# The ninth expert of a gated mixture: half of its tokens by seven block products instead of eight, and the last layers' work packed into fewer steps

## The reference, cut to what matters

```python
# layer 2: eight experts and a shared one, D = 256, F = 1024
g = einsum('bsd,edf->ebsf', h, Wg); u = einsum('bsd,edf->ebsf', h, Wu)
expert_outs = einsum('ebsf,efd->ebsd', silu(g) * u, Wd)
x2 = x + (1 - sg) * einsum('be,ebsd->bsd', probs, expert_outs) + sg * ((silu(h @ Sg) * (h @ Su)) @ Sd)
# layer 3: adapter of 64 hidden units, then a layer norm (weights picked by language)
z = x2 + relu(x2 @ w1 + b1) @ w2 + b2
x3 = x2 + (z - mean(z)) * rsqrt(var(z) + 1e-5) * gamma + beta
# layer 4: one matrix for each sequence
out = x3 + x3 @ W[subject].T + bias[subject]
```

## Time and profile before

| what | us |
|---|---|
| median of 3 runs (1583.22 to 1584.35) | 1583.36 |
| time of the profiled execution | 1581.01 |
| its span | 1579.2 |
| PE busy in the span | 1570.2 |
| DVE busy | 1133.2 |
| ACT busy | 931.4 |
| POOL busy | 671.3 |

### The profile page before, as it was taken

One profiled execution on the slowest core, in us unless ns is written; L12 is line 12 of the kernel. 1 busy time (PEld: TensorE's weight loads), 2 busy tenths in 40 slices (PEclk: granted clock), 3 DMA queues, 4 the chain that ended last, 5 costly groups with the idle time before them and its releaser, 6 DMA issues.

```text
span 1579.2 us, 22425 instructions
## 1 busy us (share of the span) xinstructions
PE 1570.2 (99%) x7916; PEld 1339.7 (85%) x7916; DVE 1133.2 (72%) x1685; ACT 931.4 (59%) x1683; POOL 671.3 (43%) x621
## 2 busy tenths in 40 slices
PE   9999999999999999999999999999999999999999
PEld 7888888999988888888888888888888888888898
DVE  6855556788889876777777776776776777657567
ACT  6655555666666665565666566656666666555444
POOL 7865544766787431432432442342342352038000
PEclk9999999999999999999999999999999999999999
DMA  4111105555520000010010010010010010022000
GB/s 161 56 53 54 54 27 179 169 183 177 171 83 31 20 34 27 14 41 27 15 40 28 14 41 27 14 40 28 14 41 27 14 41 27 15 59 77 14 14 28
DMA packets 31012, 85.98 MB, mean 54 GB/s; under 512 B 5030, under 2 KB 10534, under 8 KB 30774
## 3 DMA queue, kind: packets, MB, share of 16 engines
q1 hardware_dynamic: 30310, 83.21, 16.0%
q0 software_dynamic: 304, 1.10, 0.2%
q10 hardware_dynamic: 288, 0.26, 0.1%
HBM read 82.46 MB, written 2.10 MB: 54 GB/s over the span
## 4 chain that ended last, share of the span: by engine, by line
PE 93%; POOL 3%; issue 2%; DMA 0%; ACT 0%; DVE 0%; SPq 0%; POOLq 0%; ACTq 0%; DVEq 0%
PE up L682 13%; PE up L684 13%; PE up L683 13%; PE sum L441 12%; PE sum L442 12%; PE sum L443 12%; PE up L441 4%; PE up L442 3%; PE up L443 3%; PE up L450 2%; PE up L449 2%; PE up L451 2%; POOL expert_in L1496 1%; DMA raw<-in_shared 0%; POOL shared_up L1496 0%
## 5 line engine op out<-in xcount | busy, mean ns | idle before, releaser
L1305 ACT ACTIVATE hidden_hi<-up_tile 128x512 fp32r<-128x512 f32 x256 | 161.1, 629 | 189.2 <-DVE up_tile L2125 166.7
L2130 DVE TENSOR_TENSOR hidden_lo<-up_tile,hidden_hi 128x512 fp32r<-128x512 f32 x256 | 197.9, 792 | 44.7 <-ACT hidden_hi L1305 44.7
L2120 DVE TENSOR_TENSOR gate_tile<-up,gate_tile 128x512 f32<-128x512 f32 x192 | 130.1, 687 | 137.7 <-PE up L684 137.5
L441 PE MATMUL sum<-hidden_hi,down 128*128 128x512 f32 x512 | 199.2, 389 | 0.0
L443 PE MATMUL sum<-hidden_hi,down 128*128 128x512 f32 x512 | 199.2, 389 | 0.0
L442 PE MATMUL sum<-hidden_lo,down 128*128 128x512 f32 x512 | 199.2, 389 | 0.0
L683 PE MATMUL up<-x_sums,gate_up 128*128 128x512 f32 x512 | 199.2, 389 | 0.0
L682 PE MATMUL up<-x_sums,gate_up 128*128 128x512 f32 x512 | 199.2, 389 | 0.0
L684 PE MATMUL up<-x_sums,gate_up 128*128 128x512 f32 x512 | 199.2, 389 | 0.0
L2125 DVE TENSOR_TENSOR up_tile<-up_tile,gate_tile 128x512 f32<-128x512 f32 x192 | 184.0, 985 | 2.2
L1298 ACT ACTIVATE gate_tile<-gate_tile 128x512 f32<-128x512 f32 x192 | 119.9, 633 | 90.4 <-DVE gate_tile L2120 88.1
(11 more groups left out here) (332 smaller groups left out, 4004.9 us busy)
## 6 DMA issues: line engine op xcount, KB each, us to landing
raw<-in_experts SPq DMA_DIRECT2D x64, 512.0 KB, 3.3
raw<-in_l SPq DMA_DIRECT2D x51, 512.0 KB, 3.3
raw<-in_shared SPq DMA_DIRECT2D x23, 512.0 KB, 3.3
raw<-in_w SPq DMA_DIRECT2D x8, 256.0 KB, 2.6
x<-in_xT SPq DMA_DIRECT2D x3, 512.0 KB, 9.2
l_stage<-in_l SPq DMA_DIRECT2D x3, 512.0 KB, 4.2
out<-out_stage SPq DMA_DIRECT2D x6, 256.0 KB, 2.2
gate_w<-in_gw POOLq DMA_DIRECT2D x1, 1024.0 KB, 7.0
```

The source lines that it names most:

```text
L441: pe.matmul(out, wh, vh, start=start, stop=False)
L1305: A(hi[:, i], cu[:, i], ACT.Copy).then_inc(hi_done, 1)
L2120: V.tensor_tensor(t, ps, t, ALU.add).then_inc(c_done[m], 1)
L2130: V.tensor_tensor(lo[:, i], cu[:, i], hi[:, i].bitcast(f32), ALU.subtract).then_inc(lo_done, 1)
```

## The change

The ninth expert's first 1024 tokens go as a seventeenth row of pairs (`PAIR_BLOCKS` gets `(8, 0)`), so that 16 of the 40 plain steps go away and 4 pairs come in. The plain steps that stay are one job of 512 tokens and two of 256 (24 steps), and they read the pair's weight tiles; the one block that the pairs do not keep as such is kept in `l21` (one cast more of 128 columns on ACT and two subtractions on POOL for each pair of tiles). The separate tiles `gul` and `dnl` and their preparation go away. Units 0 and 1 (tokens 0 to 1023) are complete when the pairs are, so their stages now begin in steps 2 and 3. `WHEN` is written anew: five units' stages lie in 24 steps and the ones behind. The late weights are cast in steps 1, 1, 3, 3, 4, 5, 6, 7 (`LATE_AT`), the centring of b2 (`center_b2`, `b2_stage`) moves from step 9 to step 3. SP loads the constants before the pairs of the ninth expert, the eight b1 and four of the biases ahead of the fourth late weight, and the other four biases after unit 1's adapter down. For the units of 512 tokens ACT forms both squares and DVE only adds them. y, squares and hidden tiles have two or three copies at new places, among them squares of unit 0 at the place where the row sum of unit 1 goes, so `row_sum` waits for the variance of unit 0; on POOL it and `rstd_stage(0)` stand in the loop over the late weights. Unit 1 uses the other PSUM banks.

```diff
-LAST_JOBS = [(0, BLK), (BLK, BLK), (2 * BLK, BLK), (3 * BLK, S), (3 * BLK + S, S)]
+LAST_JOBS = [(2 * BLK, BLK), (3 * BLK, S), (3 * BLK + S, S)]
+UNITS = [(0, BLK), (BLK, BLK)] + LAST_JOBS
+LAST_STEPS = 8 * len(LAST_JOBS)
...
+PAIR_BLOCKS = [(e, j) for e in range(NS) for j in range(2)] + [(NS, 0)]
+NSS = len(PAIR_BLOCKS) * PAIRS
+LATE_AT = [1, 1, 3, 3, 4, 5, 6, 7]
...
-    (9, 10, 11, 11, 11, 11, 12, 12, 12, 13, 13, 13, 13, 14, 14, 14, 15, 15, 16, 16, 17, 18),
-    (17, 18, 19, 19, 19, 19, 20, 20, 20, 21, 21, 21, 21, 22, 22, 22, 23, 23, 24, 25, 25, 26),
-    (25, 26, 27, 28, 28, 28, 30, 30, 30, 31, 32, 31, 32, 34, 34, 35, 35, 36, 38, 38, 39, 39),
-    (34, 34, 35, 35, 35, 35, 37, 37, 37, 38, 39, 39, 40, 41, 43, 43, 45, 45, 46, 48, 46, 50))]
+    (2, 2, 4, 4, 4, 4, 6, 6, 6, 7, 7, 7, 7, 8, 8, 9, 9, 10, 12, 12, 12, 13),
+    (3, 6, 8, 9, 9, 9, 11, 11, 11, 12, 13, 12, 13, 15, 15, 15, 16, 16, 18, 18, 19, 19),
+    (10, 11, 14, 15, 15, 15, 17, 17, 17, 18, 19, 18, 19, 21, 21, 21, 22, 22, 24, 24, 26, 27),
+    (18, 18, 20, 21, 21, 21, 23, 23, 23, 24, 25, 25, 25, 26, 27, 27, 29, 29, 30, 32, 30, 34))]
...
                 act.wait_ge(centered, DT * i + 1)
-                A(sq[:, 0, c], y[:, 0, c], ACT.Square).then_inc(sq_first, 1)
+                if i:
+                    act.wait_ge(var_done, i)
+                A(sq_of[i][:, 0, c], y_of[i][:, 0, c], ACT.Square)
+                act.wait_ge(centered, DT * (i + 1))
+                A(sq_of[i][:, 1, c], y_of[i][:, 1, c], ACT.Square).then_inc(sq_first, 1)
...
             for b in reversed(range(B)):
-                hooks.setdefault(late_step(b), []).insert(0, lambda b=b: late_hi(b))
-            hooks.setdefault(24, []).append(beta_hi_part)
+                hooks.setdefault(LATE_AT[b], []).insert(0, lambda b=b: late_hi(b))
+            hooks.setdefault(16, []).append(beta_hi_part)
...
             def row_sum(i):
 
                 b0, nb, t0, c0, n = unit(i)
-                pool.wait_ge(x2_done, DT * (i + 1))
...
+                for dt in range(DT):
+                    x2_ready(pool, i, dt)
+                pool.wait_ge(mean_done, i)
+                pool.wait_ge(var_done, 1)
+                G(xst[:], x[:, 0, t0:t0 + n], x[:, 1, t0:t0 + n], ALU.add).then_inc(xs_sum, 1)
...
             for b in range(B):
                 w3_plus_one(b)
+                if b == B - 1:
+                    row_sum_lo(1)
                 if b:
                     late_lo(b - 1)
+                if b == 6:
+                    row_sum(1)
+                    rstd_stage(0)
             late_lo(B - 1)
...
-            hooks.setdefault(9, []).append(center_b2)
+            hooks.setdefault(16, []).append(beta_lo_part)
+            hooks.setdefault(3, []).append(center_b2)
```

More of the change, by code:

```diff
@@ L63 @@
 del WHEN[0]["hid"]
-WHEN += [{"x2": 42, "up": 43, "hid": 44, "down": 45, "res": 46, "square": 46, "split": 47, "var": 47, "eps": 49,
-          "scaled": 48, "base": 51, "final": 52, "beta": 41}]
+WHEN += [{"x2": 26, "up": 27, "hid": 28, "down": 29, "res": 30, "square": 30, "split": 31, "var": 31, "eps": 33,
+          "scaled": 32, "base": 35, "final": 36, "beta": 25}]
 STAGES += ["split", "beta", "scaled", "base", "final"]
@@ L155, in build @@
     ws = [place(f"weight_sums{s}", [P, 2, 7 * P], f32, over=f"gate_up{s}", skip=7 * K1) for s in range(PAIRS)]
-    xst = place("x_row_sum", [P, BLK], f32, over="raw", skip=14336)
-    xsr = [place(f"x_row_sum_parts{r}", [P, 2, BLK], f32r, over="weights", skip=(12 - 4 * r) * K1) for r in range(2)]
+    xst = place("x_row_sum", [P, BLK], f32, over="weights", skip=14 * K1)
+    xsr = place("x_row_sum_parts", [P, 2, BLK], f32r, over="weights", skip=12 * K1)
     cg = place("gate_tile", [P, 3, BLK], f32, over="weights", skip=88 * K1)
@@ L282, in last_steps @@
         def last_steps(step, hooks):
-            for T in range(40):
+            for T in range(LAST_STEPS):
                 job = T // FT
@@ L774, in last_up @@
                         b = (0, 1, 3, 2)[f % 2 * 2 + dt]
-                        c = slice(b * P, (b + 1) * P)
-                        last = product(ps, gul[f // 2][:, 0, m, c], gul[f // 2][:, 1, m, c],
+                        wt = [l21[f // 2][:, h, m] if b == 3 else gu[f // 2][:, h, m, b * P:(b + 1) * P] for h in range(2)]
+                        last = product(ps, wt[0], wt[1],
                                        xh[:, dt, tok:tok + N], xl[:, dt, tok:tok + N], dt == 0, dt == DT - 1)
@@ L973, in _ @@
                 l0_block(tb)
[L974 to L977, removed]
+            for e, j in PAIR_BLOCKS:
+                for s in range(PAIRS):
+                    pair_up(e, j, s)
             hooks = placed({"up": l2_up_stage, "mean": mean_stage, "down": l2_down_stage, "var": var_stage,
@@ L995, in _ @@
             last_steps(last_step, hooks)
-            for T in range(40, 60):
-                if T < 42:
+            for T in range(LAST_STEPS, ALL_STEPS):
+                if T < LAST_STEPS + 2:
                     last_down(T - 2, S)
@@ L1365, in pair_tiles @@
                     weights(e, j, s)
[L1367 to L1370, removed]
+            for e, j in PAIR_BLOCKS:
+                for s in range(PAIRS):
+                    pair_tiles(e, j, s)
             tile_hi(NSS - 1, 3)
@@ L1422, in scale_stage @@
                     for dt in range(DT):
-                        last = A(y[:, dt, c], y[:, dt, c], ACT.Copy, scale=cols[:, b, 2 + dt:3 + dt])
+                        last = A(y_of[i][:, dt, c], y_of[i][:, dt, c], ACT.Copy, scale=cols[:, b, 2 + dt:3 + dt])
                 last.then_inc(y_scaled, 1)
@@ L1750, in _ @@
                 mixed_lo_part(NB - 2, dt)
-            for e in range(NS):
+            for e in range(NE1):
                 weight_sums(e, 2)
@@ L2362, in out_stage @@
                 dve.wait_ge(l3_done, 2 * i + part + 1)
+                if i == 1 and not part:
+                    dve.wait_ge(mean_done, 3)
                 if i >= 2 and not part:
                     dve.wait_ge(stored[i % 2], 32 * (i // 2))
+                    dve.wait_ge(small_full, 16 * late_small)
                 V.tensor_tensor(ostage[:, i % 2, q:q + half],
```

258 lines of the change are left out of this document (132 added, 126 removed).

## The result

The changed kernel takes 1602.56 us (median of 4 runs, 1601.44 to 1603.53), the one before 1583.29 us beside it (4 runs, 1582.88 to 1584.35). The ratio is 1.0124, with a 95% interval of 1.0112 to 1.0136: slower by 19.3 us. I had forecast slower, 12.7 us, in a range that ends at 1603, 0.4 us above what was measured. The profiled execution took 1602.16 us, with a span of 1600.4.

A forecast was written before the change was run, and what follows sets the result against it. PE was taken to bound the kernel, time being the sum of its issue distances. Stalls of 18.6 us less 5.4 for products and 0.5 for a gap gave +12.7: 1583.4 to 1596.1 us on the median, range 1583 to 1603.

The forecast's parts named there:

- my own forecast: Whole kernel: stalls outweigh the saved products, +12.7 us, 1596.1 on the median; own range 1589 to 1600.5, chance 0.62.
- the third rival: PE's clock falls to 1.2 GHz in the 8.5 us rest before unit 0's broadcast: +5.1 us, 1601; chance 0.15.
- The products: PE's matmuls: 16 plain steps (65.3 us) go out, four pairs (59.8 us) come in, 24 matmuls fewer: -5.4 us.
- The moved loads: SP's 12 small loads issued before the fourth late weight, which isn't cast before step 3: no cost.
- Stall one: Step 4: PE waits for `center_b2` on DVE, needed for unit 0's mean: 3.0 us, bounds 1 to 4.5.
- the walk: The four engines' lists followed in order, step by step, with profiled durations, noting a stall where PE finds its operand missing.
- Stall two: Step 8: PE waits for unit 0's diagonals, behind a 12.2 us chain from the variance: 8.5 us, bounds 7 to 10.
- Stall three: Steps 11 and 12: PE waits for tile 9 (0.75) and unit 1's hidden tile (3.2): 4 us, bounds 2 to 6.
- The rest: On to step 25: many waits below 1 us where three units meet, 3.1 us in sum, bounds 0 to 5.
- the covered gap: PE's 0.2 us wait before the last unit's broadcast, now covered by unit 2's layer 4: -0.5 us in all.
- the tail: What follows step 25: claimed to keep its shape, so no change in time.
- The rivals that end lower: Two: PE stays full, 1577.5 us, chance 0.15; or stalls sum to some 6 us, 1583.5, chance 0.08.

The follow-up runs named there:

- experiment 9: Changed kernel with the small loads (b1, bias) back in their old order, each behind its own late weight: 1607.83 us, ratio 1.0165.
- experiment 1: Changed kernel with ACT's high part of unit 1's row sum moved from behind step 6 to behind step 7: 1601.67 us, ratio 1.0121.
- experiment 2: Changed kernel with the cast of the eighth late weight (and its centring) moved from step 7 to step 8: 1599.36 us, ratio 1.0103.
- experiment 3: Changed kernel with the moves of experiment 1 and experiment 2, and POOL's exponent of unit 0 ahead of unit 1's row sum: 1594.81 us, ratio 1.0069.
- experiment 4: Changed kernel with 28 extra, unused 512-column matmuls on PE while it waits before unit 0's broadcast: 1603.39 us, ratio 1.0127.
- experiment 5: Changed kernel with `center_b2` moved to the front of DVE's work behind step 3: 1598.21 us, ratio 1.0087.
- experiment 6: Changed kernel with the edits of experiment 3 and experiment 5 together: 1591.67 us, ratio 1.0052.
- experiment 7: On experiment 6, unit 0's add, split of x and its low part one step later: 1594.25 us, ratio 1.0071.
- experiment 8: On experiment 6, unit 0's variance and the stages after it, unit 1's row sum and the last late weight a step later: 1591.49 us, ratio 1.0049.
- experiment 11: On experiment 7, layer 4 of unit 0 moved to step 13 and its second store to 14: 1593.06 us, ratio 1.0060.
- experiment 12: On experiment 8, unit 0's epsilon a step earlier (7) and its low part of x in step 12: 1591.34 us, ratio 1.0054.

## Why the prediction was right, and where its sizes were off

The direction and the mechanism held: the three stalls came where they were forecast, at the engines that were named. The number held in part by luck. 1602.56 lies 2.1 us above the range of my own forecast (1589 to 1600.5) and nearest to the third rival's 1601, to which I had given 0.15; only the wider range for rivals, up to 1603, covers it.

**The products.** Right. The first matmul of two successive pairs of the ninth expert (first block product behind the pair's start):

```profile
1418.43 0.39 PE L722 MATMUL up<-x_hi,gate_up 128*128 128x512 f32 x1
...
1433.39 0.39 PE L722 MATMUL up<-x_hi,gate_up 128*128 128x512 f32 x1
```

14.96 us, as in the earlier trace rows, with no wait in the stage. The moved loads held nothing back, and experiment 9 shows what they would have held in the old order.

**Stall one** (3.0, bounds 1 to 4.5) measured 4.7, above the upper bound, where the walk itself had given 2.6. The walk was right in its order; the DVE terms in it were too short. The timeline of DVE:

```profile
1481.33 2.65 DVE L2269 TENSOR_TENSOR x_lo<-x,x_hi 128x512 fp32r<-128x512 f32 x2
...
1489.76 1.89 DVE L2269 TENSOR_TENSOR x_lo<-x,x_hi 128x512 fp32r<-128x512 f32 x2 [1.89 <-ACT x_hi L1421]
...
1492.57 1.28 DVE L2258 TENSOR_SCALAR minus_mean<-ones 128x128 fp32r<-128x128 f32 x1
```

The same pair of subtractions takes 1.29 us where POOL has nothing to do. I had seen the 2.54 in the earlier trace rows and put it in the bound and not in the sum, although POOL is busy for 9.12 of 10 us here. I also used 0.76 for `minus_mean`, which took 1.28. Against the walk the first pair of subtractions costs 1.3 us more, the second 0.6 and `minus_mean` 0.5.

**Stall two** (8.5, bounds 7 to 10) measured 7.8, and experiments 1 to 3 show its links one by one. **Stall three** (4.0) measured 3.5 in waits and 4.0 in distances. **The rest** (3.1) is 4.7 less the 2.5 that the kernel before had of such small pieces, 2.2.

**The sum failed in one step**: it had the stalls without the clock. The third rival, to which I gave 0.15, was a part of the truth, and came twice: 2.5 us behind stall one and 1.8 behind stall two, 4.3 in all (4.5 with both corrections from above), where I had priced it once at 5.1. I had tied the fall to the 8.5 us rest alone; the 4.7 us rest sufficed. The page "TensorE: Matmul & The Clock Gate" of the Trainium skill (section "What's actually happening") says that the clock follows how busy PE has lately been; the traces agree, with 0.43 for 0.227 us behind a rest of 4.7, and with full rate when the rest is filled (experiment 4). But not each rest has its fall: behind stall three (3.0 us) the clock stayed up in the changed kernel and in experiments 2 and 5, and fell in experiments 1, 3, 4 and 6. In those four a part of the gain was paid back there.

Between the profiled executions 21.2 - 12.7 = 8.5 us were missing. By distances they are: the clock 4.3, stall one 4.9 - 3.0 = 1.9, stall two 8.0 - 8.5 = -0.5, stall three 4.0 - 4.0 = 0, the rest 2.2 - 3.1 = -0.9, the 0.5 for the covered gap that are in this rest already, the tail 0.7 (I had said that it keeps its shape), and 2.1 before step 0: 8.1 in all, 8.7 with the broadcast's 0.6. On the medians 6.6 were missing, since the profiled execution before lay 2.3 below its median and the one after 0.4.

Of the 2.1 before step 0, 1.3 is a slow stretch at 311 us, which 12 of the 13 profiled executions of changed kernels have and the one before hasn't; it lies ahead of all that the change touches. The change isn't needed for such a fall, and isn't shown to cause it. Experiment 9 has the change and not the slow stretch. And of 30 later executions of the kernel before, four have a mean granted clock of 1.000 and took 1580.5 to 1581.3 us; the other 26 have 0.998 or 0.999 and took 1581.5 to 1585.5. So the one profiled (clock 1.000, 1581.01 us) was one of the few without a fall, and that fits with the profiled executions lying further apart than the medians.

**The rivals that end lower** were wrong. PE didn't stay full even with the chain undone. Undoing the waits by order gives back 1602.6 - 1591.7 = 10.9 us; what stays, 8 to 9 us above before, comes with waits for DVE and the half-rate matmuls behind them, which five variants of the table (6 to 8, 11 and 12) only moved. That a table exists in which they vanish wasn't ruled out: I didn't try spreading unit 1's and 2's stages to later steps.

## What to carry to other kernels

Taking 16 steps of 4.08 us out of the engine that bounds won 5.4 us of its work, and took 65 us of steps away under which the other engines' stages had lain. Count the cover as a quantity of its own, and for each wait in the new order ask which in-order queue it closes to a ring: here a 1.29 us row sum on POOL stood in front of PE's broadcast through eleven further links. And when a wait is taken out, expect the next one: in most of the repairs here the gain was what the wait behind it left over.

## What was unexpected of the hardware

A rest of 4.7 us brings PE to half rate for its next 12 matmuls of 512 columns (0.43 us apart). A fall can also come without any rest: at 311.6 us of the changed kernel's trace matmuls of 256 columns, back to back, go from 0.12 to 0.21 us apart for 3 us, some 2 us behind narrow products of 8 and 2 columns. The kernel before and experiment 9 have the same narrow products in their traces and no such stretch, so they don't decide it alone:

```profile
309.45 1.03 PE L670 MATMUL sum<-x,gate_w 128*128 128x2 f32 x8
...
311.38 0.28 PE L483 MATMUL sum<-hidden,expert_out 128*128 128x256 f32 x1
311.50 0.33 PE L481 MATMUL sum<-hidden,expert_out 128*128 128x256 f32 x1
311.63 0.42 PE L482 MATMUL sum<-hidden,expert_out 128*128 128x256 f32 x1
311.84 0.42 PE L483 MATMUL sum<-hidden,expert_out 128*128 128x256 f32 x1
```

Rests of 2.5 us (before unit 0's variance) brought half rate in experiments 5, 6 and 11 and not in 7.

DVE's subtraction of two SBUF tiles of 512 columns takes 0.65 us alone and up to 1.3 beside POOL (a pair 1.29 against 2.65), while its gating product with one operand in PSUM stays at 0.69. The Trainium skill (SBUF — State Buffer, "Who interferes with whom") says that a DVE instruction with two SBUF inputs contends with GpSimd reading SBUF, and that one with at most one such input, outside DVE's two-port modes, doesn't; the subtractions and the gating product agree with both halves. The 1.28 us of `minus_mean` against 0.76 stay unexplained: POOL was busy beside both.
